# A mixture of experts by routed token lists: scatter by expert, 23 tiles with register-addressed weights, accumulating scatter into the output

## The reference, cut to what matters

```python
# x: (4, 256, 128), ctx: (4, 256, 128)
x = x + xattn(layernorm(x), ctx, ctx)   # 16 heads of 8, causal, ALiBi bias
# feed-forward on T = 1024 tokens, 8 experts, top 2
h = layernorm(x).reshape(T, 128)
probs = softmax(h @ gate_w + gate_b)
top_w, top_idx = top_k(probs, 2)
top_w = top_w / sum(top_w)
combine = zeros((T, 8)); combine[t, top_idx] = top_w
hid = silu(einsum('td,edf->tef', h, w1)) * einsum('td,edf->tef', h, w3)   # f = 512
out = einsum('ted,te->td', einsum('tef,efd->ted', hid, w2), combine)
return x + out
```

## Time and profile before

| | |
|---|---|
| median of 3 runs | 258.41 us (257.93 to 258.68) |
| span of the profiled execution | 256.9 us |
| TensorE busy | 242.6 us, 94% |
| VectorE, ScalarE, GpSimd busy | 180.9, 145.9, 167.3 us |
| last attention matmul of `values` | 110.6 us |
| gate's last matmul | 119.5 us |
| last matmul of `down` | 251.0 us |
| DMA moved | 13.25 MB, 12.54 MB read from HBM |

### The profile page before, as it was taken

How to read it: one execution, slowest core, us unless ns; L and a number is a source line. 1 busy time by engine, 2 the same in 40 slices (tenths; PEclk the granted TensorE clock), 3 DMA queues, 4 the chain that set the end, 5 groups by cost and what they waited for, 6 DMA issues and landing times.

```text
span 256.9 us, 4759 instructions
## 1 busy us (share of the span) xinstructions
PE 242.6 (94%) x1472; PEld 191.6 (75%) x1472; DVE 180.9 (70%) x379; ACT 145.9 (57%) x241; POOL 167.3 (65%) x192
## 2 busy tenths in 40 slices
PE   6979999999999999499998899999999999999992
PEld 6647777777777777497776688888888888888871
DVE  4898376887797679946682959477676666776464
ACT  3365456848576688246863565655557555555540
POOL 5695055844745556815565788887886888877751
PEclk9995599999999999899999999999999999999999
DMA  7999100100000000000004020200100102002002
GB/s 199 301 384 314 47 1 1 41 0 0 11 9 0 0 3 0 0 3 1 0 8 163 0 83 0 75 8 0 82 0 0 82 0 82 0 3 82 0 0 82
DMA packets 10140, 13.25 MB, mean 52 GB/s; under 512 B 1040, under 2 KB 6160, under 8 KB 10128
## 3 DMA queue, kind: packets, MB, share of 16 engines
q1 hardware_dynamic: 9984, 12.63, 15.0%
q10 hardware_dynamic: 144, 0.48, 0.6%
HBM read 12.54 MB, written 0.56 MB: 51 GB/s over the span
## 4 chain that ended last, share of the span: by engine, by line
PE 36%; POOL 25%; issue 20%; DVE 9%; DMA 4%; ACT 1%; POOLq 1%; SPq 0%; DVEq 0%; ACTq 0%
POOL hl L879 22%; PE banks L343 6%; PE banks L388 6%; PE banks L391 5%; PE banks L368 4%; PE banks L355 4%; PE banks L336 3%; POOL acc L886 3%; PE banks L407 2%; DVE x_norm L1048 2%; PE banks L399 2%; DMA comb_all<-c_dram 2%; DMA cf<-in_consts 1%; DVE neg_max L979 1%; DMA c_dram<-comb_t 1%
## 5 line engine op out<-in xcount | busy, mean ns | idle before, releaser
L879 POOL TENSOR_TENSOR hl<-hid,hh 128x512 fp32r<-128x512 f32 x62 | 84.1, 1363 | 26.8 <-ACT hh L713 26.7
L1122 DVE TENSOR_TENSOR hid<-silu,banks 128x512 f32<-128x512 f32 x64 | 43.9, 685 | 37.4 <-POOL hl L879 26.4
L705 ACT ACTIVATE silu<-banks 128x512 f32<-128x512 f32 x64 | 38.3, 598 | 50.9 <-PE banks L563 50.8
L811 POOL TENSOR_TENSOR p_low<-probs,p_high 128x768 fp32r<-128x768 f32 x16 | 29.6, 1851 | 38.1 <-ACT p_high L653 38.1
L561 PE MATMUL banks<-xh,wh 128*128 128x512 f32 x128 | 51.0, 399 | 0.7 <-DVE hid L1122 0.7
L562 PE MATMUL banks<-xl,wh 128*128 128x512 f32 x128 | 50.8, 397 | 0.0
L563 PE MATMUL banks<-xh,wl 128*128 128x512 f32 x128 | 50.7, 396 | 0.0
L713 ACT ACTIVATE hh<-hid 128x512 fp32r<-128x512 f32 x64 | 40.0, 625 | 4.6 <-DVE hid L1122 4.5
L388 PE MATMUL banks<-p_high,v_pad 128*72 128x256 f32 (+1 forms) x128 | 30.8, 285 | 0.1
L652 ACT ACTIVATE probs<-banks 128x768 f32<-128x768 f32 x32 | 26.1, 814 | 8.1 <-PE banks L372 7.7
L561 PEld LDWEIGHTS banks<-xh,wh 128*128 128x128 f32 x128 | 24.0, 188 | 7.4 <-DVE wl L1155 1.1
(11 more groups left out here) (102 smaller groups left out, 403.0 us busy)
## 6 DMA issues: line engine op xcount, KB each, us to landing
comb_all<-c_dram SPq DMA_DIRECT2D x8, 512.0 KB, 3.7
w_sb<-in_L_ffn_w SPq DMA_DIRECT2D x2, 1536.0 KB, 12.3
w_sb<-in_L_ffn_w SPq DMA_DIRECT2D x3, 512.0 KB, 6.8
k_in<-in_ctx SPq DMA_DIRECT2D x4, 128.0 KB, 4.2
v_in<-in_ctx SPq DMA_DIRECT2D x4, 128.0 KB, 3.1
out<-x_norm SPq DMA_DIRECT2D x2, 256.0 KB, 2.5
cf<-in_consts ACTq DMA_DIRECT2D x1, 466.0 KB, 3.8
x_in<-in_x SPq DMA_DIRECT2D x1, 384.0 KB, 4.8
```

Source lines behind the costliest of these rows:

```text
L705: nc.scalar.activation(silu[k % 2][:], g_ps[k % 2], ACT.Silu)\
L811: nc.gpsimd.tensor_tensor(p_low[g % 2][0][:], probs[0][:], p_high[g % 2][0][:].bitcast(F32), ALU.subtract)\
L879: nc.gpsimd.tensor_tensor(hl[k % 4][:], hid[k % 2][:], hh[k % 4][:].bitcast(F32), ALU.subtract).then_inc(hl_done[k % 4], 1)
L1122: nc.vector.tensor_tensor(hid[k % 2][:], silu[k % 2][:], u_ps[k % 2], ALU.mult)\
```

## The change

1. **Routing.** After the gate VectorE marks the chosen two experts of each token (`chosen`). TensorE ranks the tokens within each expert by nine small matmuls with a triangle and ones (`rank`). VectorE makes of the ranks a row number for each of the 2048 token copies in a DRAM list `slots` (8 x 1024 rows and 7 x 128 more, 576 bytes each: token, weights, token number), and a table of 23 tiles of 128 rows: which expert's weights, which first row. 23 is 2048/128 + 7, enough for any distribution; where a list ends within a tile, pad rows fill it, with weight 0 and a token number past the output.
2. **Pads.** ACT writes pad rows over all of `slots` by one DMA before its first exponential.
3. **Scatter.** POOL issues 16 indirect DMAs, each of 128 rows of `xm`. `xm` (tokens, weights, number) takes the place of `x_norm` here.
4. **Gather.** SP waits for all 16, then for each tile loads the first row's number into a register and issues a DMA of 128 rows.
5. **Tiles.** Tokens are stationary and weights move: six matmuls of 512 columns, four transposes of `hid`, four pairs of 256 and 128 columns for w2, with the weights' columns addressed by a register (`own`). ACT and VectorE split in place of POOL.
6. **Output.** SP stores `x_mid` and zeros first; POOL adds each tile's rows to it by an indirect DMA with addition, each after the one before has landed.
7. **Weights.** All 24 blocks are split in the attention stage, one per group in the loop, two per group in the last batch, six after it, in place in one tensor `weights` (high and low); the splits on VectorE are gone.

The diff, cut:

```diff
+            act.wait_ge(route_in, 16)
+            act.dma_start(slots.rearrange("(n p) c -> p n c", p=P),
+                          pad_row.unsqueeze(1).broadcast_to([P, SLOT_ROWS // P, ROW]))\
+                .then_inc(pads_in, 16)
...
+                    if not last_one:
+                        act.wait_ge(w_first_in, 16 * 4)
+                        act.wait_ge(w_in, 16 * 8)
+                        high_weights(GROUPS * b + g)
+                    elif g < GROUPS - 1:
+                        for i in range(2):
+                            high_weights(LOOP_UNITS + 2 * g + i)
...
+            sp.wait_ge(rows_ready, 1)
+            sp.wait_ge(slots_out, 16 * TILES * TOP_K)
+            for t in range(SLOT_TILES):
+                first = sp.value_load(tile_row[0:1, t:t + 1], min_val=0,
+                                      max_val=SLOT_ROWS - SLOTS)
+                sp.dma_start(xs[:, t, :], slots[ds(first, SLOTS), :]).then_inc(xs_in[t], 16)
...
+            pe.wait_ge(chosen_ready, 1)
+            rank()
+            keep_clock(40)
+            pe.wait_ge(table_ready, 1)
+            pe.wait_ge(w_split, W_UNITS)
+            turn_slots(0)
+            own = {}
+            for t in range(SLOT_TILES + 2):
+                if t < SLOT_TILES:
+                    own[t] = up(t)
+                if t + 1 < SLOT_TILES:
+                    turn_slots(t + 1)
+                if 0 <= t - 1 < SLOT_TILES:
+                    turn_hidden(t - 1)
+                if t >= 2:
+                    down(t - 2, own[t - 2])
...
+            for t in range(TILES):
+                for k in range(TOP_K):
+                    nc.gpsimd.indirect_dma_start(
+                        out=slots, out_offset=bass.IndirectOffsetOnAxis(place_i[:, t, k:k + 1], 0),
+                        in_=xm[:, t, :], in_offset=None).then_inc(slots_out, 16)
+
+            pool.wait_ge(base_out, 32)
+            for t in range(SLOT_TILES):
+                pool.wait_ge(y_done, t + 1)
+                if t:
+                    pool.wait_ge(out_sem, 16 * t)
+                nc.gpsimd.indirect_dma_start(
+                    out=out, out_offset=bass.IndirectOffsetOnAxis(
+                        xs[:, t, TOKEN_COL:TOKEN_COL + 1].bitcast(I32), 0),
+                    in_=y[t % 3][:], in_offset=None, compute_op=ALU.add).then_inc(out_sem, 16)
+            pool.wait_ge(out_sem, 16 * SLOT_TILES)
...
+            def result(t):
+
+                dve.wait_ge(y_low_done, t + 1)
+                if t >= 3:
+                    dve.wait_ge(out_sem, 16 * (t - 2))
+                nc.vector.scalar_tensor_tensor(y[t % 3][:], y_ps[:, 0:D],
+                                               slot_w[:, t:t + 1], y_low[t % 2][:],
+                                               ALU.mult, ALU.add).then_inc(y_done, 1)
+
+            def slot_weights(tiles):
+
+                for t in tiles:
+                    dve.wait_ge(xs_in[t], 16)
...
+            low_slots(0)
+            for t in range(SLOT_TILES + 2):
+                if t < SLOT_TILES:
+                    multiply(t)
+                if t == 0:
+                    slot_weights(range(EARLY))
+                if t == 2:
+                    slot_weights(range(EARLY, SLOT_TILES))
+                    dve.wait_ge(slot_w_done, 2)
+                if t + 1 < SLOT_TILES:
+                    low_slots(t + 1)
+                if 0 <= t - 1 < SLOT_TILES:
+                    low_hidden(t - 1)
+                if t >= 2:
+                    result(t - 2)
```

605 lines of the change are left out of this document (317 added, 288 removed).

## The result

The changed kernel takes **291.88 us** (median of four runs, 289.74 to 297.74); the kernel before took 258.17 us beside it (four runs, 256.89 to 258.68). The ratio is 1.127 (95% interval 1.117 to 1.136). The forecast was 268 us, slower by 3.7%; it is slower by 12.7%. Executions of one kernel differ by several us with the TensorE clock that each was granted (289.74 us came with a mean clock of 0.815, 297.74 us with 0.773), so where an experiment is worth less than that I go by milestones in its profile, not by its median. The kernel before lies between 253.3 and 266.2 us wherever it was measured, its medians between 258.0 and 259.2.

The account below looks back on a forecast made before the run. TensorE's dense expert matmuls were taken to bound the kernel. Forecast: 110.6 + attention 11 + routing 17 + scatters 21.5 + gathers 24 + first result 1.5 + tiles 80.5 = 266.1, plus 0.3 and 1.5: 268 us, range 240 to 303.

Parts of the forecast that it names:

- routing: Serial stretch from the last attention matmul to the row numbers `placed`: 17 us (16 to 19).
- gathers: SP's 23 gathers, each with register load, three small instructions and issue: 0.95 us apiece.
- Rival 1: Small DMAs are cheap, so TensorE's 3.4 us tile decides: 246 us, faster; chance 0.27.
- Rival 4: TensorE stays at 1.2 GHz in the tiles after idling, 5.4 us a tile: 311 us; chance 0.07.
- the even scatters: Sign in the tiles: POOL's output scatters evenly 3.5 us apart to the end.
- The wait for the last gather: Sign: VectorE at `slot_prob` waits for the last gather, 15 us or more.
- 1.2 + 2.3 = 3.5 us: Output scatters: POOL's issue plus landing sets each tile's step; 23 steps make 80.5 us.
- 3.4 us: TensorE's time per expert tile: up matmuls, five transposes, four pairs in down, 0.2 us for waits.
- Weight splits inside the attention loop: ACT copies and POOL subtractions delay the loop: 1 us for each of three batches, 2.5 us in the last.
- the weight wait, 6.5 us: First loop pass: pads delay weights, ACT waits 6 us; TensorE loses 5 of that plus 1.5 at half clock.
- Sum 11 us: Attention stage in all: -1 + 6.5 + 3 + 2.5 us, between 3 and 19.
- 24 us, and the first result 1.5 us later: VectorE at tile 2 waits for all 23 gathers: 23 x 0.95 + 2.3 us, 12 to 48, before any output scatter.

Follow-up runs that it names:

- The plain scatter: Changed kernel with POOL's output scatters made without addition, same waits and bytes: 281.89 us.
- The two outputs: Changed kernel with even and odd tiles added to separate DRAM outputs, each scatter waiting for the one two before, one final sum by DMA: 277.2 us.
- the other order: Changed kernel with the loop's weight splits moved to groups 0, 1 and twice 2, none in group 3: 287.64 us.

## Why the prediction was right and wrong

**The direction and the structure were right.** The 146.3 us of dense work became a row of serial DMAs; the stages came in the order and nearly with the prices forecast: routing 18.2 us for 17, POOL's issue 1.26 us for 1.2 (0.96 busy, 0.30 between), landing 2.3 for 2.3, gathers 1.08 each for 0.95. Rival 1, cheap DMAs, was to decide under 0.95 us an issue, and neither issue is. Rival 4, a clock that stays low in the tiles, didn't come: 1.00 from 230 to 260 us. Of the signs that the prediction named, the even scatters came, at 4.0 us in place of 3.5, and TensorE was busy for under 80% after 150 us (54%; 81% in the tiles alone, from 206 to 280 us). The wait for the last gather was 13.85 us for 15 or more, and ScalarE waited 2.7 us, not 6 (up to 5.1 in other profiles).

**The step that failed: "1.2 + 2.3 = 3.5 us" for POOL's accumulating scatter.** The mechanism was right and the term mis-sized: it is 4.14 us (4.05 to 4.20 in the runs). Two things are wrong in it. I added the issue to the landing, but the profile's time to landing counts from the start of the issue; behind it stands a gap of 0.75 us that I didn't have. And I priced the addition at nothing, though my own argument against rival 1 said that it reads before it writes. The plain scatter shows 2.2 + 0.8 = 3.0 us, the one with addition 3.3 + 0.75 = 4.0, and two longer steps make the mean 4.14: the addition is 1.0 us. So 3.5 was too high for the plain scatter and too low for this one, and that it came as near as it did is luck: a term too much and two missing. 22 x 0.64 = 14 of the 17.1 us; the other 3 are the end behind the last landing on POOL's queue. The Trainium skill's figure for a DMA from POOL ("DMA: Bandwidth & Descriptors", Anatomy of one DMA) is about 2.0 us fixed plus the bytes at 436 GB/s; by it I estimate 2.15 us for these 64 KB. The plain scatter's landing agrees with that, at 2.2 us. The step of a chain is longer all the same, 3.0 us, by the 0.8 us to the next issue, and the addition takes the landing to 3.3 us; neither is in that figure. The prediction had said that by the page, with nothing added for the addition, the step would be TensorE's; without the addition TensorE is full indeed, with 3.0 us an even step.

**TensorE's tile was mis-sized too, and that was hidden.** "3.4 us" is 2.86 us: the five transposes take 0.46 us where I had 0.75, `down` 0.96 for 1.04, and the 0.2 us of waits aren't there. Since 3.4 stood so close to 3.5, I took the choice between the two for nearly even, and a mis-sized ring for cheap. It was the largest single loss: 4.14 against 2.86, 28 us over 22 tiles. The two outputs, a small edit, take 26.9 us of it back, and 21.2 after the final sum is paid.

**"Weight splits inside the attention loop", 3 + 2.5 us, and the weight wait, 6.5 us.** Sum 11 us; with the clock kept from 50 us on 9.8 us (120.2 against 110.4). That the two lie so close is in part luck, since the shares are others: without the splits the stage is 5.7 us shorter where I had 1, and the splits with the wait for the weights cost 15.5 us where I had 12. Of these, 10.7 are up to the second pass's keys, where I had some 7.5, 1.8 in the second pass for 1, and 3.0 behind it for 3.5. The wait for the weights itself is worth 0.4 to 2.1 us where ScalarE waits 2.2 us (the other order), and 2.03 us of TensorE's time and a lower clock behind it where it waits 4.05; my 6.5 us for it isn't shown, nor excluded for that case. I had seen that POOL makes the keys ahead of `p_low` with 0.53 us of slack, and counted the delay once, 1 us a batch. It is 0.93 + 1.14 us of TensorE's time.

**What had no term at all: the clock.** 7.6 us in the profiled execution (127.8 - 120.2), and, by my estimate from the times above, next to nothing in the runs of 289.74 and 290.08 us. I had the earlier trace rows at hand, where an idle of TensorE is followed by 0.50, and used it for the tiles (rival 4), not for the loop, where an added wait stands in a stage that is full at 1.00.

**"24 us, and the first result 1.5 us later"** came out as 29.1: the last gather lands 26.3 us after the first issue (1.08 each, 1.8 to land), and the first scatter comes 2.8 us behind it for 1.5: five VectorE operations in a row, from `slot_prob` at 195.10 to `y`, which ends at 196.95, and 0.8 us to POOL's issue. That the wait is paid in full was right (13.8 us).

## What to carry to other kernels

Where each step of a serial DMA chain waits for the landing of the last, the step is issue, landing and gap together, and it is to be compared with the compute engine's bare need for a step, not with a rounded-up one; splitting the target so that neighbours needn't wait is worth trying first. Work put "beside" a full engine is free only if it isn't ahead of something that engine waits for within the same pass: look at what its queue does next. And a full stage that runs at full clock can lose more than the wait itself: here 2 us of waits were followed by half clock in most profiles, and in one not.

## What the runs showed of the hardware

- Indirect scatter of 128 rows from POOL: 0.96 us to issue plus 0.30 to the next, 2.2 to 2.3 us to land; with the addition 1.55 us and 3.2 to 3.4 us. A POOL that waits for the landing issues again 0.75 us behind it. Beside VectorE's subtractions the issues keep their pace (1.26 us).
- The same stage with the same waits ran, from 50 to 100 us, at 1.00 in one profiled execution and at 0.73 to 0.80 in five others; 14 idle matmuls ahead of each wait kept it at 1.00 in the one that was profiled, and its four runs lie within 4.2 us (7.7 for the kernel beside it). Why one execution kept its clock without them stays open.
- SP's register load, three small instructions and issue: 1.08 us (23 in 24.8 us), 0.33 of it the issue.
- Additions into two tensors in turn overlap: 2.86 us a step, which is TensorE's time for a tile, where into one they take 4.14.
- Behind the last landing on POOL's queue the span goes on for 3.6 to 3.7 us; behind SP's last store for 0.5 us (one run).
